# A graph network on one core: the encoder's steps without a gap, its early sums earlier, and eight source tiles of a layer's second sum moved forward

## The chip, the cores and the metric

The kernel runs on one core of a Trainium2 chip. The metric is the device time in microseconds (us) of that core, the median of several runs. The engines are PE (TensorE: matrix products, with weight loads shown as PEld), DVE (VectorE), ACT (ScalarE), POOL (GpSimd) and SP (SyncE, which here issues most DMAs; its DMA issues stand as SPq in the profile). Each engine runs its own program in order and waits on semaphores for the others.

## What is computed

3125 nodes with 128 features go through two graph networks, one after the other. Only the first is touched by the change. Cut to what matters (each edge adds its source's row to its target's row):

```python
h = relu(layernorm(x))
h = relu(h @ enc_w1.T + enc_b1) @ enc_w2.T + enc_b2          # the encoder
for w in conv_w:                                             # 5 layers
    agg = segment_sum((h @ w)[src], dst)
    gi, gh = agg @ gru_wih.T + gru_bih, h @ gru_whh.T + gru_bhh
    r, z = sigmoid(gi_r + gh_r), sigmoid(gi_z + gh_z)
    n = tanh(gi_n + r * gh_n)
    h = (1 - z) * n + z * h
x = x + sigmoid(decoder(relu(h)))
x = x + second_network(relu(layernorm(x)))                   # two sparse sums, 128 to 256 to 128
```

## The kernel before, in words

The graph is held as a dense matrix of edge counts, `AT` (source by target, fp8), so that each sum over edges is a row of matrix products. There are 25 **tiles** of up to 128 source nodes (`T`, the last, `FT` = 24, has 53), and 7 **chunks** of 4 tiles as targets (`NC` = 7, `TC` = 4; chunks 0 to 5 have 512 nodes, chunk 6 has 53). A sum for one chunk takes 49 products: every tile's state is split in a high and a low half (`H16`, f16), the last tile's stand in one. Sums are counted over the layers by q = layer x 7 + chunk.

**The first stage** builds `AT` in 40 **blocks** (b = 0 to 39, `NBT`) of 16 windows. In block b the DVE compares keys into one-hot matrices (`onehots(b)`, the pair of L877 instructions), the PE multiplies them (`windows(b)`, L1205, 16 products; it waits for `onehots_ready` >= b+1), and the ACT copies the counts into `AT` (L1583, two instructions, written out behind the products). The DVE may be up to 4 blocks ahead. Other work is hung on these blocks by hand-written tables:

- The encoder's steps. `step(b)` tells which of 16 steps stands in block b. In step 2s the PE transposes chunk s of the input (L1226) and multiplies chunk s-1 by the second weight (`enc2`, L1234, into the bank `EC2`, PSUM bank 7). In step 2s+1 it multiplies chunk s by the first weight (`enc1`, L1239) and transposes the encoded chunk s-1 (L1247). The ACT has a copy or an activation behind each (L1637, L1620, L1630, L1642). Before, step b+1 stands in blocks -1 to 6, block 7 (`REST`) has none, and step b stands in blocks 8 to 15.
- The DVE's share, placed by `block_of`, the inverse of `step`: statistics of chunk n (`first_norm(n)`: L839, L842, L851, then a power on POOL, L733) behind `onehots` of block `block_of[2n] - 2`, its normalization (L894) one block later, and the low half of an encoded chunk (`low_encoded(n)`, L903) behind `onehots` of `block_of[2n + 5]`. Each such piece stands ahead of the next block's `onehots` on the DVE.
- Keys. `KEYS_AT = {5: 1, 12: 2, 20: 3, 28: 4}`: the DVE works out a set of 128 key columns in block 5, 12, 20, 28 (L860 to L867); the PE transposes it one block later (`transposed_keys`, L1193, into the same bank `EC2`), and the ACT copies it out (`copied_keys`, L1597) behind that block's copy of the counts. An `enc2` product writes that bank, so it waits until all sets whose block lies before its own are copied:

```python
pe.wait_ge(keys_copied, 1 + sum(k < block_of[off] for k in KEYS_AT))
nc.tensor.matmul(PS[EC2][:, 0:w1], enc2, rS[:, 0:w1], start=True, stop=True).then_inc(enc2_product, 1)
```

- Sums of the first layer, as far as their sources are encoded: `PART[b]` lists `(q, t0, t1)`, the tiles t0 to t1-1 of sum q, put behind the encoder's step of block b (L1342, two products a tile). In all, the 40 blocks hold the sums 0 to 3 and a part of sum 4, in both versions.

The PE's order in a block is: windows, a transpose of keys if there is one, the encoder's step, a product of combined weights (blocks 2 to 6, L1214), the parts of sums.

**The layers.** For layers 1 to 4 the sum of chunk 0 (`aggregate`, L1260) takes its sources in groups of 4 tiles as they arrive by DMA transposes from `yS` to `H16` (L604 and L607 for chunks 0 to 5, L611 for chunk 6; semaphores `state_moved[0]` to `[6]`). Ahead of group g, `between(g)` may put other work: at g = 2 the gates of the last chunk of the layer before (`gates`, L1273 to L1284). Then comes the sum of chunk 1, then the gates of chunk 0, and so on. Two PSUM banks take turns for the sums.

Of the kernel before, what the change touches and what calls it, by code (L numbers as in the profile page):

```python
# [5 lines left out]
def gnn_kernel(nc, x, src, dst, edges, row_ends, enc_w1T, enc_b1, enc_w2T, enc_b2, conv_wT, gru_wihT, gru_whhT,  # L6
# [10 lines left out]
    P = 128  # L17
    GP = 125
    PM = GP // 16 * 16
    T = N // GP  # L20
# [37 lines left out]
    TC = 4  # L58
    CH = [(t, min(TC, T - t)) for t in range(0, T, TC)]
    NC = len(CH)  # L60
    width = lambda c: min(TC * P, N - TC * P * c)
# [11 lines left out]
    with ctx:  # L73
# [118 lines left out]
        def late(shape, dt):  # L192
            size = {F32: 4, I32: 4, F16: 2, BF16: 2}[dt]
            n = size
            for d in shape[1:]:
                n *= d
            v = carve(AT, p2[0], shape, dt)
            p2[0] += (n + 31) // 32 * 32
            return v
# [11 lines left out]
        CHECKED = 4  # L211
        FLAGGED = 20
        EARLY = 3
        OUT = late([P, TL, F], F32)
        dinvO = late([P, TL], F32)
        V16 = H16[:, 0, :, :, :]
# [6 lines left out]
        def spare(r, shape, dt):  # L223
            n = 2 if dt == F16 else 4
            for d in shape[1:]:
# [16 lines left out]
        AGG, RB, ZB, NB, IB, TB, CB = (0, 1), 2, 3, 4, 5, 6, 7  # L242
        AHEAD = 4
        ENC = -1
        REST = 7
        step = lambda b: b - ENC - (b > REST) if b != REST else None
        block_of = {step(b): b for b in range(ENC, NBT)}
        KEYS_AT = {5: 1, 12: 2, 20: 3, 28: 4}
        ROWS_AT = {7: 2, 11: 3, 15: 4}
        assert all(b + 1 < k * (PW // J) for b, k in KEYS_AT.items())  # L250
        PART = {7: [(0, 0, 4)], 8: [(0, 4, 8)], 10: [(0, 8, 12)], 12: [(0, 12, 14)], 13: [(0, 14, 16)], 14: [(0, 16, 20)],
                15: [(1, 0, 4)], 16: [(0, 20, 24)], 17: [(1, 4, 8)], 18: [(0, 24, T), (1, 8, 11)]}
        PART.update({19: [(1, 11, 14)], 20: [(1, 14, 18)], 21: [(1, 18, 21)], 22: [(1, 21, T)]})
        EVEN = [0, 4, 7, 11, 14, 18, 21, T]
        PART.update({23 + 7 * i + g: [(2 + i, EVEN[g], EVEN[g + 1])] for i in range(2) for g in range(7)})
        PART.update({37 + g: [(4, EVEN[g], EVEN[g + 1])] for g in range(NBT - 37)})
        BEGUN = EVEN[NBT - 37]
        COMB = [2 + l for l in range(L)]
        assert max(PART) < NBT
        for q in range(AHEAD + 1):  # L260
            done = [(t0, t1) for b in sorted(PART) for q1, t0, t1 in PART[b] if q1 == q]
            assert [t0 for t0, _ in done] == [0] + [t1 for _, t1 in done][:-1] and done[-1][1] == (T if q < AHEAD else BEGUN)
        EA, EB, EC2 = 6, 1, 7
        agg_bank = lambda q: PS[(0, TB, 1, CB)[q] if q < AHEAD else AGG[q % 2]]
# [30 lines left out]
        sum_ready = sem("sum_ready"); sum_copied = sem("sum_copied"); hidden_product = sem("hidden_product")  # L295
# [262 lines left out]
        def _(sp):  # L558
# [96 lines left out]
            def stored(p0, p1, u0, n0, n1):  # L655

                r = u0[1] - u0[0]
                sp.dma_start(out[n0:n1, :].rearrange("(i r) f -> i r f", r=r), OUT[p0:p1, u0[0]:u0[1], :]).then_inc(output_stored, 16)

# [40 lines left out]
        def _(pool):  # L700
# [62 lines left out]
            def low_half(c):  # L763

                pool.wait_ge(input2_hi_early, c + 1) if c < EARLY else pool.wait_ge(input2_hi, c + 1 - EARLY)
                for u0, nu, k in parts(c):
# [4 lines left out]
            for c, (t0, nt) in enumerate(CU):  # L771
                if c == 3:
                    for c1 in range(EARLY):
                        low_half(c1)
# [18 lines left out]
        def _(dve):  # L793
# [227 lines left out]
            def output_tile(u):  # L1021

                bank = PS[TILES[u % STARTED]]
                dve.wait_ge(sum2_ready, u + 1)
                link(nc.vector.scalar_tensor_tensor(OUT[:, u, :], bank[:, 0:F], dinvO[:, u:u + 1], X32[:, u, :],
                                                    ALU.mult, ALU.add))
                nc.vector.scalar_tensor_tensor(OUT[:, u, :], bank[:, F:2 * F], dinvO[:, u:u + 1], OUT[:, u, :],
                                               ALU.mult, ALU.add).then_inc(output_ready, 1)

            def decoded_tail():  # L1030
# [21 lines left out]
                for u in range(FLAGGED):  # L1052
# [11 lines left out]
                    if u == FG - 1:  # L1064
                        dve.wait_ge(sum2_transposed, 1)
                        for j in range(2):
                            k = rows2(2 * FG + j)
                            last = nc.vector.scalar_tensor_tensor(
                                OUT[0:k, 2 * FG + j, :], PS[IB][0:k, j * F:j * F + F], dinvU[0:k, 2 * FG + j:2 * FG + j + 1],
                                X32[0:k, 2 * FG + j, :], ALU.mult, ALU.add)  # L1070
# [74 lines left out]
            new_gate_input(q0 + NC - 2, NC - 2)  # L1145
            high_half(EARLY)
            new_state(q0 + NC - 2, NC - 2)
# [26 lines left out]
        def _(pe):  # L1174
# [72 lines left out]
                        last = nc.tensor.transpose(PS[EB][0:cols.shape[1], j * F:(j + 1) * F], cols, ident[:, :])  # L1247
                    last.then_inc(encoded_transposed, 1)

            def aggregate(bank, w, n0, l, ready=None, between=None):  # L1250

                for t in range(T):
                    if between is not None and t % TC == 0:
                        between(t // TC)
                    if ready is not None and t % TC == 0:
                        pe.wait_ge(*ready(t // TC))
                    if t == FT and l == 0:
                        pe.wait_ge(tail_doubled, 32 * (n0 // (TC * P) + 1))
                    for h in range(2 if t < FT else 1):
                        last = nc.tensor.matmul(bank[:, 0:w], H16[:, l % 2, t, h, :], AT3[:, t, n0:n0 + w],  # L1260
                                                start=(t == 0 and h == 0), stop=(t == T - 1))
                return last

            def gates(l, q, c):

                n0, w = CH[c][0] * P, width(c)
                H = HT[:, n0:n0 + w]
                cl = comb[:, l % 2, :]

                if q == 0:  # L1270
                    pe.wait_ge(weights_loaded, 8 * 16)
                pe.wait_ge(reset_gate, q) if q else pe.wait_ge(window_bank_free, NGR)
                nc.tensor.matmul(PS[RB][:, 0:w], whh[:, 0:F], H, start=True, stop=False)  # L1273
                pe.wait_ge(update_gate, q) if q else pe.wait_ge(window_bank_free, NGR)
                nc.tensor.matmul(PS[ZB][:, 0:w], whh[:, F:2 * F], H, start=True, stop=False)  # L1275
                pe.wait_ge(reset_hidden, q) if q else pe.wait_ge(window_bank_free, NGR)
                nc.tensor.matmul(PS[NB][:, 0:w], whh[:, 2 * F:G], H, start=True, stop=True).then_inc(hidden_product, 1)  # L1277
                pe.wait_ge(sum_copied, q + 1)
                if c == 0:
                    pe.wait_ge(comb_loaded[l % 2], 16 * (l // 2 + 1))  # L1280
                nc.tensor.matmul(PS[RB][:, 0:w], cl[:, 0:F], aggS[:, 0:w], start=False, stop=True).then_inc(reset_product, 1)  # L1281
                nc.tensor.matmul(PS[ZB][:, 0:w], cl[:, F:2 * F], aggS[:, 0:w], start=False, stop=True).then_inc(update_product, 1)  # L1282
                pe.wait_ge(new_input, q) if q else None
                nc.tensor.matmul(PS[IB][:, 0:w], cl[:, 2 * F:G], aggS[:, 0:w], start=True, stop=True).then_inc(input_product, 1)  # L1284
# [28 lines left out]
            def last_chunks(l):  # L1313

                def step(g):
                    if g == 2:
                        gates(l, (l + 1) * NC - 1, NC - 1)
                return step


# [28 lines left out]
            for b in range(NBT):  # L1349
# [5 lines left out]
                if b in COMB:  # L1355
                    combine(COMB.index(b))
                for q, t0, t1 in PART.get(b, []):
                    aggregate_part(q, t0, t1)


            for l in range(L):
                for c in range(NC):
                    q = l * NC + c
                    if q == AHEAD:
                        aggregate_part(q, BEGUN, T)
                    if AHEAD < q:
                        n0, w = CH[c][0] * P, width(c)
                        if q >= 2:
                            pe.wait_ge(sum_copied, q - 1)
                        ready = between = None  # L1370
                        if c == 0 and l >= 1:
                            ready = lambda g: (state_moved[g], (32 if g < NC - 1 else 16) * l)
                            between = last_chunks(l - 1)
                        aggregate(agg_bank(q), w, n0, l, ready=ready, between=between).then_inc(sum_ready, 1)
                    if l == L - 1 and 2 <= c < NC - 1:
                        decode1(c - 2)
                    if 1 <= c <= NC:
                        gates(l, q - 1, c - 1)
                    if l == L - 1 and c == 1:
                        permute_scales()  # L1380
                    if l == L - 1 and c == NC - 1:
                        decode1(c - 2)
                    if l == L - 1 and 2 <= c < NC - 1:
                        decode2(c - 2)
# [120 lines left out]
            n0, w = CH[NC - 1][0] * P, width(NC - 1)  # L1505
# [25 lines left out]
        def _(act):  # L1531
# [174 lines left out]
            for l in range(L):  # L1706
                for c in range(NC + 2 if l < L - 1 else NC):
# [29 lines left out]
                    if l == L - 1 and 2 <= c < NC:  # L1737
                        decode_sig(c - 2)
                        if c == NC - 2:
                            act.wait_ge(sum_ready, L * NC)  # L1740
                            for c1 in range(EARLY):
                                u0, nu = CU[c1]
# [82 lines left out]
```

## Time and profile before

| | us |
|---|---|
| median of 3 runs | 737.01 (736.59 to 737.25) |
| the profiled execution | 736.87 |
| its span in the trace | 735.0 |
| PE busy in the span | 720.2 |
| DVE busy | 331.2 |
| ACT busy | 316.5 |
| granted clock | 0.999 |

The profiled execution is 1.87 us longer than its span, and 0.14 us below the median. The span is cut by the work: up to about 125 us the 40 blocks; from there to 565.5 us the five layers; then the decoder and the second network. PE busy counts the product's own duration with its pipeline; where the PE is never starved, the starts of its instructions tell the pace better than their durations.

### The profile page before, as it was taken

To read this page: it belongs to the slowest core of one execution; us is meant where nothing else is said; L and a number is where in the kernel's file an instruction comes from. 1 tells how busy PE (TensorE), PEld (TensorE's weight loads), DVE (VectorE), ACT (ScalarE), POOL (GpSimd) and SP (SyncE) were. 2 spreads that over 40 slices of the span, in tenths; PEclk is the share of its full clock that TensorE was granted. 3 is DMA by queue.
4 is the path that set the end of the run, shared out by engine and by line. 5 is a ranking of instruction groups with operands and counts; after the bars stand their busy time and mean duration, and the time that the engine had idled before them with its cause. 6 is when DMAs were issued, how large, how long until landed. Compare 5 with 4: busy or idle time off the path is not lost.

```text
span 735.0 us, 9911 instructions
## 1 busy us (share of the span) xinstructions
PE 720.2 (98%) x4071; PEld 394.7 (54%) x4071; DVE 331.2 (45%) x665; ACT 316.5 (43%) x467; POOL 43.6 (6%) x57
## 2 busy tenths in 40 slices
PE   6989999999999999999999999999999999999998
PEld 4556666445444444444444444544445545558887
DVE  7999997625023241123331222655644642122532
ACT  5978877736244344234452333433446421122000
POOL 4230000000000000000000000120002220000000
PEclk9999999999999999999999999999999999999999
DMA  6020000835003222021230213520001100000100
GB/s 170 3 92 10 3 4 3 156 62 84 8 1 62 62 47 45 1 48 38 53 78 0 49 37 38 94 86 2 1 0 54 53 1 1 1 1 3 37 25 31
DMA packets 79239, 28.39 MB, mean 39 GB/s; under 512 B 70519, under 2 KB 78390, under 8 KB 79062
## 3 DMA queue, kind: packets, MB, share of 16 engines
q1 hardware_dynamic: 78230, 26.93, 17.3%
q8 instruction: 33, 0.54, 0.3%
q0 software_dynamic: 240, 0.66, 0.3%
q10 hardware_dynamic: 720, 0.13, 0.1%
q14 instruction: 16, 0.13, 0.1%
HBM read 8.03 MB, written 2.60 MB: 14 GB/s over the span
## 4 chain that ended last, share of the span: by engine, by line
PE 89%; DVE 6%; DMA 2%; ACT 1%; SPq 1%; issue 0%; POOL 0%; ACTq 0%; DVEq 0%
PE PSA L1260 35%; PE PSA L1477 9%; PE PSA L1421 8%; PE PSA L1342 7%; PE PSA L1205 4%; PE PSA L1273 4%; PE PSA L1282 4%; PE PSA L1281 4%; PE PSA L1277 4%; PE PSA L1275 4%; PE PSA L1284 3%; DVE CT L877 3%; PE PSA L1409 2%; PE PSA L1397 1%; DMA H<-yS 1%; PE PSA L1301 1%
## 5 line engine op out<-in xcount | busy, mean ns | idle before, releaser
L1260 PE MATMUL PSA<-AT,H 128*128 128x512 fp8e3 (+1 forms) x1470 | 275.8, 347 | 0.3 <-DMA H<-yS 0.2
L1260 PEld LDWEIGHTS PSA<-AT,H 128*128 128x128 f16 x1470 | 126.7, 98 | 151.5 <-issue 12.0
L1090 DVE SCALAR_TENSOR_TENSOR rS<-PSA,bias,rS 128x512 f32<-128x512 f32 (+1 forms) x35 | 23.9, 682 | 261.1 <-ACT rS L1659 261.1
L1659 ACT ACTIVATE rS<-PSA,bias 128x512 f32<-128x512 f32 (+1 forms) x35 | 22.1, 632 | 198.0 <-PE PSA L1281 197.9
L1583 ACT ACTIVATE AT<-PSA 128x1000 fp8e3<-128x1000 f32 (+1 forms) x79 | 74.5, 999 | 18.6 <-PE PSA L1205 18.3
L1557 ACT ACTIVATE CTL<-AT 128x3125 fp8e3<-128x3125 fp8e3 (+1 forms) x25 | 69.9, 2797 | 0.0
L1421 PE MATMUL PSA<-CT,H 128*128 128x512 fp8e3 (+1 forms) x336 | 65.3, 351 | 0.1
L1477 PE MATMUL PSA<-AT,CT 128*128 128x256 f16 x576 | 64.9, 273 | 0.0
L1477 PEld LDWEIGHTS PSA<-AT,CT 128*128 128x128 fp8e3 x576 | 55.5, 98 | 6.5 <-issue 0.2
L1342 PE MATMUL PSA<-AT,H 128*128 128x512 fp8e3 x245 | 58.0, 379 | 0.0
L1205 PEld LDWEIGHTS PSA<-CT 128*128 128x128 bf16 x625 | 40.2, 99 | 16.3 <-DVE CT L877 8.9
L877 DVE TENSOR_TENSOR CT<-CT 128x2048 bf16<-128x2048 bf16 x40 | 48.6, 1215 | 0.0
L1205 PE MATMUL PSA<-CT 128*128 128x125 bf16 x625 | 44.6, 224 | 3.5 <-DVE CT L877 3.5
L1421 PEld LDWEIGHTS PSA<-CT,H 128*128 128x128 f16 x336 | 29.4, 98 | 33.9 <-issue 1.9
L877 DVE TENSOR_TENSOR CT<-yS,CT 128x2000 bf16<-128x2000 bf16 x40 | 47.6, 1191 | 0.0
L1342 PEld LDWEIGHTS PSA<-AT,H 128*128 128x128 f16 x245 | 23.1, 98 | 23.8 <-issue 2.3
L1273 PE MATMUL PSA<-HT,whh 128*128 128x512 f32 (+1 forms) x70 | 32.7, 548 | 0.0
L1277 PE MATMUL PSA<-HT,whh 128*128 128x512 f32 (+1 forms) x70 | 32.6, 547 | 0.0
L1284 PE MATMUL PSA<-aggS,comb 128*128 128x512 f32 (+1 forms) x70 | 32.6, 547 | 0.0
L1281 PE MATMUL PSA<-aggS,comb 128*128 128x512 f32 (+1 forms) x70 | 32.6, 547 | 0.0
L1275 PE MATMUL PSA<-HT,whh 128*128 128x512 f32 (+1 forms) x70 | 32.6, 547 | 0.0
L1282 PE MATMUL PSA<-aggS,comb 128*128 128x512 f32 (+1 forms) x70 | 32.6, 547 | 0.0
(186 smaller groups left out, 662.3 us busy)
## 6 DMA issues: line engine op xcount, KB each, us to landing
AT<-scale_scratch SPq DMA_DIRECT2D x1, 1562.5 KB, 6.5
H<-in_x SPq DMA_DIRECT2D x1, 1536.0 KB
out<-AT SPq DMA_DIRECT2D x12, 128.0 KB
comb_scratch<-CT SPq DMA_DIRECT2D x1, 960.0 KB, 4.6
comb<-comb_scratch SPq DMA_DIRECT2D x5, 192.0 KB, 2.6
H<-yS SPq DMA_TRANSPOSE x48, 2.5
H<-in_x SPq DMA_DIRECT2D x1, 512.0 KB, 5.0
CT<-AT SPq DMA_TRANSPOSE x25, 4.0
```

The lines of the kernel that those rows point to most:

```text
L877: last = nc.vector.tensor_tensor(oh, io.unsqueeze(1).to_broadcast([SL, GW, n_, 2]), pairs.unsqueeze(2).to_broadcast([SL, GW, n_, 2]), ALU. ...
L1205: last = nc.tensor.matmul(PS[2 + 2 * g + w // 4][:, (w % 4) * 128:(w % 4) * 128 + W * T], ohP[b % BL][:, j // 2, :, j % 2], ohK[b % BL][:, ...
L1260: last = nc.tensor.matmul(bank[:, 0:w], H16[:, l % 2, t, h, :], AT3[:, t, n0:n0 + w], start=(t == 0 and h == 0), stop=(t == T - 1))
L1273: nc.tensor.matmul(PS[RB][:, 0:w], whh[:, 0:F], H, start=True, stop=False)
L1275: nc.tensor.matmul(PS[ZB][:, 0:w], whh[:, F:2 * F], H, start=True, stop=False)
L1277: nc.tensor.matmul(PS[NB][:, 0:w], whh[:, 2 * F:G], H, start=True, stop=True).then_inc(hidden_product, 1)
L1281: nc.tensor.matmul(PS[RB][:, 0:w], cl[:, 0:F], aggS[:, 0:w], start=False, stop=True).then_inc(reset_product, 1)
L1342: last = nc.tensor.matmul(agg_bank(q)[:, 0:w], H16[:, 0, t, h, :], AT3[:, t, n0:n0 + w], start=(t == 0 and h == 0), stop=(t == T - 1))
L1421: nc.tensor.matmul(PS[bank][:, 0:w], halves[:, u, h, :], CT2[:, u // 2, n0:n0 + w, u % 2], start=(u == 0 and h == 0), stop=False)
L1477: nc.tensor.matmul(PS[TILES[u % STARTED]][:, 0:2 * F], CT2[:, s // 2, nodes(u), s % 2], Z16[:, s, :, :].rearrange("p h f -> p (h f)"), sta ...
L1557: nc.scalar.activation(junk[0:k, :], AT3[0:k, t, 0:N], ACT.Copy, saturate=False, accum_out=deg[0:k, t:t + 1]).then_inc(degree_summed, 1)
L1583: nc.scalar.activation(AT3[0:P, :, w0 * W:(w0 + gw) * W].rearrange("p t (w d) -> p t w d", w=gw), counts[:, 0:gw, 0:W * T].rearrange("p w ...
```

## The change

In the first stage block 7 is no longer left out: step b+1 stands in block b for all 16 steps, so the steps 8 to 15 come one block sooner (blocks 7 to 14), and with them the DVE's pieces for chunks 4 to 6 and the low halves of chunks 2 to 6. The table `PART` follows: its parts of sums 0 and 1 are cut differently and end in blocks 17 and 22. In the layers 1 to 4 the first 8 tiles of the sum of chunk 1 (16 products) are issued ahead of the sixth group (g = 5) of the sum of chunk 0; the sum of chunk 1 then takes the rest (33 products) at its old place.

```diff
+        EARLY_TILES = 2 * TC
...
-        REST = 7
-        step = lambda b: b - ENC - (b > REST) if b != REST else None
+        step = lambda b: b - ENC
...
-        PART = {7: [(0, 0, 4)], 8: [(0, 4, 8)], 10: [(0, 8, 12)], 12: [(0, 12, 14)], 13: [(0, 14, 16)], 14: [(0, 16, 20)],
-                15: [(1, 0, 4)], 16: [(0, 20, 24)], 17: [(1, 4, 8)], 18: [(0, 24, T), (1, 8, 11)]}
-        PART.update({19: [(1, 11, 14)], 20: [(1, 14, 18)], 21: [(1, 18, 21)], 22: [(1, 21, T)]})
+        PART = {7: [(0, 0, 4)], 8: [(0, 4, 8)], 9: [(0, 8, 12)], 11: [(0, 12, 16)], 13: [(0, 16, 20)], 14: [(1, 0, 4)],
+                15: [(0, 20, 24)], 16: [(1, 4, 8)], 17: [(0, 24, T), (1, 8, 10)]}
+        PART.update({18 + i: [(1, 10 + 3 * i, 13 + 3 * i)] for i in range(5)})
...
-            def aggregate(bank, w, n0, l, ready=None, between=None):
+            def aggregate(bank, w, n0, l, ready=None, between=None, t0=0, t1=T):
...
-                for t in range(T):
+                for t in range(t0, t1):
...
                 def step(g):
                     if g == 2:
                         gates(l, (l + 1) * NC - 1, NC - 1)
+                    if g == NC - 2:
+                        q = (l + 1) * NC + 1
+                        pe.wait_ge(sum_copied, q - 1)
+                        aggregate(agg_bank(q), width(1), CH[1][0] * P, l + 1, t1=EARLY_TILES)
                 return step
...
-                        aggregate(agg_bank(q), w, n0, l, ready=ready, between=between).then_inc(sum_ready, 1)
+                        aggregate(agg_bank(q), w, n0, l, ready=ready, between=between,
+                                  t0=EARLY_TILES if c == 1 and l >= 1 else 0).then_inc(sum_ready, 1)
```

Three places show how the instructions move. The lines of the changed file are 5 higher behind `aggregate` (L1342 is L1346, L1583 is L1588).

The PE in block 13 and at the begin of block 14, before (L1193 is the transpose of key set 2, L1239 and L1247 the encoder's step 13, L1234 with 53 columns its step 14):

```order
L1193 MATMUL PSA<-ident,CT 128x128 [waits keys_ready,state_encoded]
L1193 MATMUL PSA<-ident,CT 128x128
L1239 MATMUL PSA<-aggS,CT 128x53 [waits x_copied]
L1247 MATMUL PSA<-ident,HT 128x128 [waits encoded_lo,state_encoded]
L1247 MATMUL PSA<-ident,HT 128x128 x3
L1342 MATMUL PSA<-AT,H 128x512 [waits encoded_lo]
L1342 MATMUL PSA<-AT,H 128x512 x3
L1205 MATMUL PSA<-CT 128x125 [waits window_bank_free,onehots_ready]
```

The same place now:

```order
L1193 MATMUL PSA<-ident,CT 128x128 [waits keys_ready,state_encoded]
L1193 MATMUL PSA<-ident,CT 128x128
L1234 MATMUL PSA<-rS,CT 128x53 [waits keys_copied,state_encoded,enc1_relu]
L1346 MATMUL PSA<-AT,H 128x512 [waits encoded_lo]
L1346 MATMUL PSA<-AT,H 128x512 x7
L1205 MATMUL PSA<-CT 128x125 [waits window_bank_free,onehots_ready]
```

Step 13 has gone to block 12, step 14 has come up from block 14, and it now stands directly behind the transpose of the keys, with the wait for `keys_copied`.

The DVE behind block 5's keys (L867 is the last of them), before:

```order
L867 SCALAR_TENSOR_TENSOR CT<-CT 128x128 [waits starts_subtracted]
L877 TENSOR_TENSOR CT<-CT 128x2048 [waits windows_counted]
L877 TENSOR_TENSOR CT<-yS,CT 128x2000
L839 BN_STATS stat<-H 128x6 [waits x_loaded1]
L839 BN_STATS stat<-H 128x6 x3
L842 BN_AGGR mv<-stat 128x2 [waits vector_chain]
L842 BN_AGGR mv<-stat 128x2 x3
L851 TENSOR_SCALAR mv<-mv 128x4 [waits vector_chain]
L903 SCALAR_TENSOR_TENSOR H<-PSA,H 128x4x128 [waits encoded_hi]
```

The same place now:

```order
L867 SCALAR_TENSOR_TENSOR CT<-CT 128x128 [waits starts_subtracted]
L839 BN_STATS stat<-H 128x6 [waits x_loaded1]
L839 BN_STATS stat<-H 128x6 x3
L842 BN_AGGR mv<-stat 128x2 [waits vector_chain]
L842 BN_AGGR mv<-stat 128x2 x3
L851 TENSOR_SCALAR mv<-mv 128x4 [waits vector_chain]
L877 TENSOR_TENSOR CT<-CT 128x2048 [waits windows_counted]
L877 TENSOR_TENSOR CT<-yS,CT 128x2000
L894 TENSOR_SCALAR H<-H,mv,lnsc 128x128 [waits roots_ready]
L894 TENSOR_SCALAR H<-H,mv,lnsc 128x128 x3
L903 SCALAR_TENSOR_TENSOR H<-PSA,H 128x4x128 [waits encoded_hi]
```

The statistics of chunk 4 now stand ahead of block 6's one-hots, and its normalization right behind them.

The PE at a layer's begin, before:

```order
L1260 MATMUL PSA<-AT,H 128x512 [waits state_moved4]
L1260 MATMUL PSA<-AT,H 128x512 x7
L1260 MATMUL PSA<-AT,H 128x512 [waits state_moved5]
L1260 MATMUL PSA<-AT,H 128x512 x7
L1260 MATMUL PSA<-AT,H 128x512 [waits state_moved6]
L1260 MATMUL PSA<-AT,H 128x512 [waits sum_copied]
L1260 MATMUL PSA<-AT,H 128x512 x48
```

And now:

```order
L1260 MATMUL PSA<-AT,H 128x512 [waits state_moved4]
L1260 MATMUL PSA<-AT,H 128x512 x7
L1260 MATMUL PSA<-AT,H 128x512 [waits sum_copied]
L1260 MATMUL PSA<-AT,H 128x512 x15
L1260 MATMUL PSA<-AT,H 128x512 [waits state_moved5]
L1260 MATMUL PSA<-AT,H 128x512 x7
L1260 MATMUL PSA<-AT,H 128x512 [waits state_moved6]
L1260 MATMUL PSA<-AT,H 128x512 [waits sum_copied]
L1260 MATMUL PSA<-AT,H 128x512 x32
```

16 of the 49 products of chunk 1's sum stand ahead of the wait for the sixth chunk's state.

## Rows read from the trace of the kernel before

**Rows 1.** The page's busy times: us, share of the span, instructions.

```profile
PE 720.2 (98%) x4071; PEld 394.7 (54%) x4071; DVE 331.2 (45%) x665; ACT 316.5 (43%) x467; POOL 43.6 (6%) x57
```

**Rows 2.** Timeline of PE, blocks 7 to 15: start, us, instruction, [idle before, releaser].

```profile
37.65 1.13 PE L1205 MATMUL PSA<-CT 128*128 128x125 bf16 x16 [0.88 <-DVE CT L877]
38.61 1.89 PE L1342 MATMUL PSA<-AT,H 128*128 128x512 fp8e3 x8
41.40 1.12 PE L1205 MATMUL PSA<-CT 128*128 128x125 bf16 x16 [0.90 <-DVE CT L877]
42.36 0.60 PE L1226 MATMUL PSA<-ident,H 128*128 128x128 f32 x4
...
43.66 1.89 PE L1342 MATMUL PSA<-AT,H 128*128 128x512 fp8e3 x8
45.39 1.11 PE L1205 MATMUL PSA<-CT 128*128 128x125 bf16 x16
...
48.91 1.13 PE L1205 MATMUL PSA<-CT 128*128 128x125 bf16 x16 [1.06 <-DVE CT L877]
...
58.43 1.12 PE L1205 MATMUL PSA<-CT 128*128 128x125 bf16 x16
59.39 0.39 PE L1193 MATMUL PSA<-ident,CT 128*128 128x128 f32 x2
59.61 0.32 PE L1239 MATMUL PSA<-aggS,CT 128*128 128x53 f32 x2
...
60.23 1.03 PE L1342 MATMUL PSA<-AT,H 128*128 128x512 fp8e3 x4
61.27 1.13 PE L1205 MATMUL PSA<-CT 128*128 128x125 bf16 x16
62.23 0.37 PE L1234 MATMUL PSA<-rS,CT 128*128 128x53 f32 x2
62.45 1.89 PE L1342 MATMUL PSA<-AT,H 128*128 128x512 fp8e3 x8
64.17 1.11 PE L1205 MATMUL PSA<-CT 128*128 128x125 bf16 x16
```

**Rows 3.** Timeline of DVE, pieces between the one-hots of blocks 6 to 14.

```profile
33.27 0.86 DVE L839 BATCH_NORM_STATS2 stat<-H 128x6 f32<-128x128 f32 x4
...
34.67 0.68 DVE L903 SCALAR_TENSOR_TENSOR H<-PSA,H 128x512 f16<-128x512 f32 x1
35.27 1.21 DVE L877 TENSOR_TENSOR CT<-CT 128x2048 bf16<-128x2048 bf16 x1
...
37.99 1.11 DVE L894 TENSOR_SCALAR H<-H,mv,lnsc 128x128 f32<-128x128 f32 x4
39.01 1.22 DVE L877 TENSOR_TENSOR CT<-CT 128x2048 bf16<-128x2048 bf16 x1
...
58.29 0.68 DVE L903 SCALAR_TENSOR_TENSOR H<-PSA,H 128x512 f16<-128x512 f32 x1
```

**Rows 4.** Timeline of ACT: a copy of encoder input in block 8, the keys' in block 13.

```profile
44.45 0.60 ACT L1637 ACTIVATE aggS<-PSA 128x512 f32<-128x512 f32 x1
...
60.90 0.39 ACT L1597 ACTIVATE CT<-PSA 128x256 bf16<-128x256 f32 x1
```

**Rows 5.** Timeline of PE, the sums at the begin of layers 1, 3 and 4.

```profile
184.91 12.69 PE L1260 MATMUL PSA<-AT,H 128*128 128x512 fp8e3 x58 [0.22 <-DMA H<-yS]
...
373.63 17.86 PE L1260 MATMUL PSA<-AT,H 128*128 128x512 fp8e3 x82
...
470.57 18.10 PE L1260 MATMUL PSA<-AT,H 128*128 128x512 fp8e3 x82
```

**Rows 6.** Timeline of ACT at the begin of layer 1, behind the first sum.

```profile
187.55 2.80 ACT L1557 ACTIVATE CTL<-AT 128x3125 fp8e3<-128x3125 fp8e3 x1
```

**Rows 7.** Timelines of DVE and POOL around block 4: statistics, power, normalization.

```profile
26.50 1.11 DVE L894 TENSOR_SCALAR H<-H,mv,lnsc 128x128 f32<-128x128 f32 x4
...
24.42 1.91 POOL L733 TENSOR_TENSOR lnsc<-mv,mhalf 128x4 f32<-128x4 f32 x1 [5.00 <-DVE mv L851]
```

## The prediction

> **What bounds the kernel now.** The page's busy times come first: the PE is busy for 720.2 of 735.0 us [rows 1], and neither version has other products than the other (4071 are in the trace). So only time in which the PE stands still can be won or lost, and the question is where it does. The second view is the PE's timeline with its idle times. In the blocks 7 to 13 it waits for the one-hots of the DVE: 0.88, 0.90 and 1.06 us ahead of the windows of blocks 7, 8 and 10 [rows 2]. From block 14 on every product follows on the one before; the DVE is ahead by then. The third place is a layer's begin. Of layers 1 to 4, layer 1 shows 0.22 us of waiting for the DMA of the state [rows 5], and in layer 4 the same 82 products take 18.10 us where layer 3's take 17.86, so 0.24 us more [rows 5]. Layers 2 and 3 show none.
>
> **The layer's begin.** 16 products are put ahead of the wait for the sixth chunk's state. A product takes 0.216 us (8 between 43.66 and 45.39, [rows 2]), so 16 take 3.45 us, and the waits of 0.22 and 0.24 us vanish under them. That is **-0.46 us**. I look for what is late next. The last source (chunk 6's state) also has 3.45 us more. The new wait for `sum_copied` asks for the sum whose copy the gates at g = 2 have already waited for, so nothing stands behind it. The first sum's end comes 3.45 us later, and the gates that need its copy come after 33 products instead of 49: 7.1 us. In these the ACT has one copy (some 0.6 us, as its other 512-column copies [rows 4]) and one instruction of 2.80 us [rows 6], so cover of 3.7 us remains. The gates themselves stay at their old place in the count of products, and DVE, ACT and SP see them unmoved. Bounds: no gain at all if other executions have no wait there, up to some 1 us if all four layers have one like these two.
>
> **The DVE's stream in the first stage.** Nothing is added, but pieces stand ahead of earlier one-hots. From rows 3: statistics of a chunk 1.40 us (33.27 to 34.67), a low half 0.60 (34.67 to 35.27), a normalization 1.02 (37.99 to 39.01). The one-hots of block 6 come 1.40 us later (statistics of chunk 4 ahead of them). Those of block 7 come 1.02 later (the statistics were ahead of them anyway, the normalization is new). Those of block 8 come 1.40 later, and those of block 12 at their old time, since by then both orders hold the same. Block 13 has the low half of chunk 4 newly ahead, which before stood behind it at 58.29 [rows 3]: 0.60 us later.
>
> **The PE up to block 13.** Windows 7 start at 37.65 + 1.02 = 38.67. The block then holds windows 0.96 (37.65 to 38.61), the encoder's step 8 of 1.30 (42.36 to 43.66, before in block 8) and 8 products of 1.73, and ends at 42.66. Windows 8 wait for the DVE until 41.40 + 1.40 = 42.80. Before, the time from windows 8 to windows 13 was 58.43 - 41.40 = 17.03 us with 1.06 of idling in it [rows 2], so 15.97 of work. Now this stretch loses step 8 (1.30), gains step 13 (0.62, from 59.61 to 60.23) and 4 more products of a sum (0.86): 16.15 us. From 42.80 that is 58.95, just short of the DVE's 58.43 + 0.60 = **59.03**, at which windows 13 start. They start 0.60 later than before, with 0.62 + 0.86 = 1.48 us more work already done: up to here the PE is ahead by **0.88 us**. The idle times of blocks 7 to 10 are used, as the change's parts stand in them; a new one of up to 1.4 us at block 6 is paid in it.
>
> **Block 13, the new wait.** Here a step goes wrong. The `enc2` product of step 14 now stands in block 13, directly behind the transpose of key set 2, and both use bank `EC2`. Its wait counts the sets of blocks before 13, so it includes set 2, which the ACT copies only behind its two copies of block 13's counts. Before, step 14 stood one block later and windows 14 lay between; it started at 62.23 without idling [rows 2]. The ACT's copy of the keys starts 60.90 - 58.43 = 2.47 us after windows 13 start and takes 0.39 [rows 2, 4], so it ends 2.86 after. The PE reaches the product after windows 0.96 and transpose 0.22 (59.39 to 59.61), 1.18 after. It stands for 2.86 - 1.18 = **1.68 us**. Bounds: 1.5, were the ACT's result seen at the start of its next instruction, and 2.0, were the first weight load after the wait seen in full. Queued behind the wait on the PE are 8 products of sum 0, ready since long, and windows 14. The PE's rows stand in the program's order throughout, so I let none of them fill the wait. From the ACT's side nothing hangs on the PE at that moment, so the wait ends.
>
> **After it.** Before, the PE stood 61.27 - 60.23 - 4 x 0.216 = 0.18 us ahead of windows 14 [rows 2]. Now windows 14 start at 59.03 + 2.86 + 0.22 (62.23 to 62.45) + 1.73 = 63.84, and the DVE has their one-hots by 61.27, so this idle time is gone. Measured against windows 15, which before came at 64.17: the new order has still block 14's windows (0.96) to go at 63.84, then 64.80, with step 14 and 40 products of sums done in both. That is **+0.63 us** (-0.88 + 1.68 - 0.18 = +0.62, the same by the parts). Beyond, the DVE's order is the same but for a low half in block 14 and 16, the PE never waited from windows 14 on and now comes later still, so the DVE's lead grows; and the total of `PART` up to block 22 is unchanged. Nothing gives the 0.63 back.
>
> **Sum.** +0.63 - 0.46 = +0.17 us. The profiled execution's 736.87 becomes 737.04; on the median of 737.01 it is **737.2 us**. I take the rows' values for both terms.
>
> **Rivals.**
> (1) *The wait in block 13 is hidden*: the ACT copies the keys before the PE gets there, for instance since the windows 13 are held back more than I think and the PE reaches the product late. For it: the wait is one in a list of three and I infer its end from one row. Against it: the ACT's copy always follows the windows by two copies of counts, whatever moment they start. Time: the +0.63 becomes -1.06 and the sum -1.52: 735.5 us.
> (2) *The layer's gain is another*: the DMA landing varies by execution. With none of it 737.6; with 1 us 736.6.
> (3) *Slower: the ACT hands over the encoder's input too late.* In block 8 the product of step 9 waits for the ACT's copy from block 7. Before, this copy ended at 44.45 + 0.60 = 45.05, 3.65 us after its block's windows (41.40) [rows 2, 4]; now 38.67 + 3.65 = 42.32, against the PE's arrival at 42.80 + 0.96 = 43.76. The slack is 1.44 us, and it decides if the copy is later by more than that. In this case the idle times of blocks 8 and 10 (0.90 + 1.06, [rows 2]) are not won: +2.0, so 739.1 us.
> (4) *Slower: POOL's power comes late.* Statistics, one-hots and normalization of chunk 4 now follow on each other, with the power on POOL (1.91 us) beside the one-hots. The same order stands already for chunk 3: the power runs from 24.42 to 26.33, and the normalization starts at 26.50 without a wait [rows 7]. If POOL could not run beside the one-hots, the power would start behind them, the normalization and all one-hots from block 7 to 13 would be 1.9 us late, and the time 739.1 us as well.
> The Trainium skill, "SBUF — State Buffer", section on practical consequences, says that a VectorE instruction with two SBUF inputs and a GpSimd one that reads SBUF exclude each other, whoever started first keeping the port. By that rule rival 4 would be the outcome. The trace does not agree: the power at 24.42 started inside the DVE's pair and was done before it ended.
>
> **Chances.** The forecast 0.73; rival 1 0.08; rival 2 0.11 (half of it to each side); rival 3 0.05; rival 4 0.03. A difference below 0.2% (1.5 us) can't be told from none in a measurement of this kernel. Faster by more needs rival 1 with the layer's gain in full, which sits on the border: 0.05. Slower by more needs rival 3 or 4: 0.08. The rest, 0.87, lies within. The range has the forecast and rival 2 with the spread of the runs (0.3 either side), and on the low side rival 1: 735.5 to 738.3 us.
>
> **What would show it.** In the changed profile: an idle time of 1.5 to 2.0 us ahead of L1234 in block 13, put down to ACT's L1597 (copy of the keys), at about 60.2 us; windows 13 starting near 59.0 and windows 14 near 63.8; no idle time by L1205 in blocks 8 to 12 above 0.2 us; one of about 1.4 us ahead of windows 6; no wait for `yS` at L1260. The last L1205 some 0.6 us later than before. I am wrong if L1234 doesn't wait in block 13, if the PE waits for ACT's L1637 in blocks 8 or 10, or if the gates after a layer's first sum begin to wait for the ACT.

## The result and the profile after

The changed kernel took 739.56 us (median of 9 runs, 737.9 to 739.82) against 736.9 us before (9 runs, 736.59 to 737.25): a ratio of 1.003 with a 95% interval of 1.0022 to 1.0039. It is slower by some 2.7 us, where 737.2 us and a range of 735.5 to 738.3 had been forecast. The profiled execution took 739.12 us with a span of 737.3 (before 735.0).

The nine runs fall in two groups. Seven have a mean granted clock of 0.998 and lie at 739.12 to 739.82 us; two have 1.000 and lie at 737.9 and 738.32. The profiled run is of the first kind. This will turn out to be the larger part of the miss.

The page's busy times, and the PE's timeline at the places of [rows 2] (start, us, instruction, [idle before, releaser]):

```profile
PE 720.9 (98%) x4071; PEld 395.8 (54%) x4071; DVE 331.4 (45%) x665; ACT 316.6 (43%) x467; POOL 45.9 (6%) x57
```

```profile
34.63 1.13 PE L1205 MATMUL PSA<-CT 128*128 128x125 bf16 x16 [1.24 <-DVE CT L877]
...
38.49 1.13 PE L1205 MATMUL PSA<-CT 128*128 128x125 bf16 x16 [0.57 <-DVE CT L877]
...
42.63 1.12 PE L1205 MATMUL PSA<-CT 128*128 128x125 bf16 x16
...
58.86 1.29 PE L1205 MATMUL PSA<-CT 128*128 128x125 bf16 x16 [0.22 <-DVE CT L877]
59.98 0.39 PE L1193 MATMUL PSA<-ident,CT 128*128 128x128 f32 x2
62.33 0.40 PE L1234 MATMUL PSA<-rS,CT 128*128 128x53 f32 x2 [1.96 <-ACT CT L1602]
62.56 2.90 PE L1346 MATMUL PSA<-AT,H 128*128 128x512 fp8e3 x8
65.25 1.75 PE L1205 MATMUL PSA<-CT 128*128 128x125 bf16 x16
66.84 0.32 PE L1247 MATMUL PSA<-ident,nS 128*117 128x128 f32 x1
67.00 1.89 PE L1346 MATMUL PSA<-AT,H 128*128 128x512 fp8e3 x8
68.72 1.12 PE L1205 MATMUL PSA<-CT 128*128 128x125 bf16 x16
```

The waits of [rows 2] ahead of the windows of blocks 8 and 10 are gone, and one of 1.24 us ahead of windows 6 is new. In block 13 the PE waits 1.96 us ahead of L1234 for the ACT's copy of the keys. What is new against the forecast are the two lines behind it: 8 products take 2.69 us (62.56 to 65.25), where 8 of them take 1.72 from 67.00 (67.00 to 68.72), and windows 14 take 1.59 instead of 0.95. The view of stretches gives the granted clock there (columns: stretch, its length, busy us and count of PE, PEld, DVE, ACT, POOL, then the clock, DMA share, GB/s):

```profile
60.00:62.30 2.30, 0.36 (x5) 0.13 (x3) 2.30 (x3) 2.18 (x4) 0.00 (x0) 1.00 0.05 12
62.30:64.00 1.70, 1.67 (x8) 0.83 (x9) 1.70 (x3) 0.54 (x2) 0.00 (x0) 0.79 0.00 0
64.00:66.00 2.00, 2.00 (x12) 1.18 (x11) 1.96 (x5) 0.00 (x0) 1.36 (x1) 0.50 0.00 0
66.00:68.00 2.00, 2.00 (x17) 1.48 (x16) 0.62 (x1) 1.66 (x2) 0.32 (x1) 0.82 0.26 66
```

From some moment between 62.3 and 64 the granted clock is at its lower level of 1.2 GHz (0.50), and it returns between 66 and 68 us. Before that the PE had been idle for 1.96 us. In narrower stretches the clock is 1.00 up to 63.1 us and 0.50 from 63.3, so it fell about 1 us after the PE had begun to work again at 62.33: the first products behind the wait still run at full pace.

The layers' begins, to be read beside [rows 5]: no wait for `yS` is left, the 82 products take 17.86 us in layer 1 and in layer 4.

```profile
182.29 17.86 PE L1260 MATMUL PSA<-AT,H 128*128 128x512 fp8e3 x82
...
473.13 17.86 PE L1260 MATMUL PSA<-AT,H 128*128 128x512 fp8e3 x82
```

The ACT around block 13's windows (the L1588 at 57.54 belong to block 12, L1625 and L1647 to step 13, the L1588 at 59.98 to block 13, and L1602 is the copy of the keys):

```profile
57.54 1.90 ACT L1588 ACTIVATE AT<-PSA 128x1000 fp8e3<-128x1000 f32 x2 [0.79 <-PE PSA L1205]
59.32 0.31 ACT L1625 ACTIVATE rS<-PSA,bias 128x53 f32<-128x53 f32 x1
59.51 0.61 ACT L1647 ACTIVATE H<-PSA 128x512 f16<-128x512 f32 x1
59.98 1.92 ACT L1588 ACTIVATE AT<-PSA 128x1000 fp8e3<-128x1000 f32 x2
61.75 0.43 ACT L1602 ACTIVATE CT<-PSA 128x256 bf16<-128x256 f32 x1
```

**The books of the profiled execution.** At the first product of the layers (L1273) the changed kernel is 2.95 us late: it starts at 128.94, before at 125.99. I had forecast 0.63. The difference, piece by piece, from the rows above and the same view elsewhere:

| | us |
|---|---|
| forecast for the first stage | +0.63 |
| the whole stage runs earlier from block 5 on (30.32 against 30.50), where the ten traces spread from 30.32 to 31.12 | -0.18 |
| windows 13 take 1.12 instead of 0.96: their second half waits for the ACT's copy of block 12 | +0.16 |
| the wait ahead of L1234 is 2.13 (62.33 - 58.86 - 1.12 - 0.22), not 1.68 | +0.45 |
| the lower clock: 2.69 - 1.73 and 1.59 - 0.95 | +1.60 |
| windows behind the two blocks with 5 products (17 and 22) take 1.09 instead of 0.95 | +0.28 |
| sum | +2.94 |

The pieces miss the 2.95 by 0.01. The layers then give back 0.63: at the gates behind layer 4's first two sums the distance is 490.83 - 488.51 = 2.32 us, and the spans differ by 2.3.

### The profile page after: what moved, and what is told of

Its sections match the earlier page's. It is cut to its first block, busy times and chain, and to the rows that moved or that the text cites. A ratio compares the mean times of both kernels' runs of the same rounds, so it can differ in the third digit from the quotient of the medians.

```text
span 737.3 us, 9911 instructions
## 1 busy us (share of the span) xinstructions
PE 720.9 (98%) x4071; PEld 395.8 (54%) x4071; DVE 331.4 (45%) x665; ACT 316.6 (43%) x467; POOL 45.9 (6%) x57
## 4 chain that ended last, share of the span: by engine, by line
PE 88%; DVE 7%; ACT 2%; POOL 1%; issue 1%; DMA 1%; SPq 0%; ACTq 0%; DVEq 0%
PE PSA L1260 37%; PE PSA L1482 9%; PE PSA L1346 7%; PE PSA L1426 5%; PE PSA L1205 4%; PE PSA L1273 4%; PE PSA L1284 3%; PE PSA L1281 3%; PE PSA L1282 3%; PE PSA L1277 3%; PE PSA L1275 3%; DVE CT L877 2%; PE PSA L1414 2%; PE PSA L1402 1%; DVE stat L839 1%
## 5 line engine op out<-in xcount | busy, mean ns | idle before, releaser
L1588 ACT ACTIVATE AT<-PSA 128x1000 fp8e3<-128x1000 f32 (+1 forms) x79 | 74.5, 1000 | 20.8 <-PE PSA L1205 20.4
L1346 PE MATMUL PSA<-AT,H 128*128 128x512 fp8e3 x245 | 59.0, 384 | 0.0
L877 DVE TENSOR_TENSOR CT<-CT 128x2048 bf16<-128x2048 bf16 x40 | 48.7, 1217 | 0.9 <-ACT CT L1602 0.9
L877 DVE TENSOR_TENSOR CT<-yS,CT 128x2000 bf16<-128x2000 bf16 x40 | 47.7, 1192 | 0.0
L1346 PEld LDWEIGHTS PSA<-AT,H 128*128 128x128 f16 x245 | 23.2, 99 | 24.3 <-issue 2.8
L1273 PE MATMUL PSA<-HT,whh 128*128 128x512 f32 (+1 forms) x70 | 32.7, 548 | 0.0
```

The source lines that it names most:

```text
L877: last = nc.vector.tensor_tensor(oh, io.unsqueeze(1).to_broadcast([SL, GW, n_, 2]), pairs.unsqueeze(2).to_broadcast([SL, GW, n_, 2]), ALU. ...
L1346: last = nc.tensor.matmul(agg_bank(q)[:, 0:w], H16[:, 0, t, h, :], AT3[:, t, n0:n0 + w], start=(t == 0 and h == 0), stop=(t == T - 1))
L1588: nc.scalar.activation(AT3[0:P, :, w0 * W:(w0 + gw) * W].rearrange("p t (w d) -> p t w d", w=gw), counts[:, 0:gw, 0:W * T].rearrange("p w ...
```

## The experiments

The theory: the wait in block 13 is the cause, first by itself and then by the lower clock behind it; the rest of the change is a gain. The rivals: the DVE's pieces moved ahead cost it, the layers' begin costs it, or the products behind the wait are slow for another reason than the clock. Each group of four ran beside the kernel before on one chip (737.26 us in the first, 737.17 in the second), and the ratios refer to that.

**The two halves of the change.** The layer part alone:

```diff
-        step = lambda b: b - ENC
+        REST = 7
+        step = lambda b: b - ENC - (b > REST) if b != REST else None
...
(PART as before)
```

> The kernel before with the layer part of the change alone. My theory after reading both traces: the waits at the begin of layers 1 and 4 were 0.39 and 0.24 us, so it is 0.6 us faster than before (736.3 us, ratio 0.9991). The rival that the early products cost as much as they save (a late copy of the first sum) expects no difference or slower.

Measured: 736.77 us, ratio 0.9995 (0.9986 to 1.0004). The median is 0.49 us under the kernel before; by the interval that can't be told from none. In its trace the waits for `yS` are gone, and both sums take 17.86 us. In the trace of before the PE's gap in layer 1 was larger than the printed idle time: 24 products from 179.34 end their issue at 184.52, the next starts at 184.91. So the gain is 0.39 + 0.24 = 0.63 us by the traces, and they show no new wait there.

The first stage alone:

```diff
                     if g == 2:
                         gates(l, (l + 1) * NC - 1, NC - 1)
-                    if g == NC - 2:
-                        q = (l + 1) * NC + 1
-                        pe.wait_ge(sum_copied, q - 1)
-                        aggregate(agg_bank(q), width(1), CH[1][0] * P, l + 1, t1=EARLY_TILES)
```

> The first stage of the change alone, the layers as before. My theory: the whole loss is in the first stage, +2.9 us where the clock falls behind the wait in block 13: 740.1 us at a mean granted clock of 0.998, and some 1.6 us less in runs where it doesn't fall. The rival that part of the loss came from the layers expects under 739.6.

Measured: 739.54 us, ratio 1.0034 (1.0022 to 1.0046). Three runs at a clock of 0.998 lie at 740.2 to 740.34, three at 1.000 at 738.48 to 738.89. I had set the rival's bound at 739.6, and the median lies 0.06 us under it; but it falls between two groups of three, so it decides nothing. Group by group the medians are 740.25 and 738.69, and those of the whole change 739.59 and 738.11 (first measurement): with the layers as before the kernel is some 0.6 us slower, which is their gain. So the whole loss is in the first stage. The profiled execution is one at 1.000, which shows the same wait without the slow products:

```profile
62.62 0.40 PE L1234 MATMUL PSA<-rS,CT 128*128 128x53 f32 x2 [1.96 <-ACT CT L1598]
62.86 1.89 PE L1342 MATMUL PSA<-AT,H 128*128 128x512 fp8e3 x8
64.58 1.11 PE L1205 MATMUL PSA<-CT 128*128 128x125 bf16 x16
```

**The wait taken away, by two ways.** First the key set goes to block 11, so that it is copied out in block 12:

```diff
-        KEYS_AT = {5: 1, 12: 2, 20: 3, 28: 4}
+        KEYS_AT = {5: 1, 11: 2, 20: 3, 28: 4}
```

> The changed kernel with key set 2 worked out in block 11 instead of 12, so that it is copied out in block 12 and step 14 in block 13 doesn't wait for it. My theory: the wait of 2.1 us and the slower clock behind it (1.6 us) both vanish, and the gain of the filled idle times comes out: 1.2 us in the first stage and 0.6 in the layers under the kernel before, 735.2 us, clock 1.000. The rival that the loss comes from the DVE's pieces moved ahead, or from the copies of the ACT, expects it to stay above 736.9.

Measured: 736.04 us, ratio 0.9985 (0.9976 to 0.9994). The wait is gone (L1234 at 60.08, directly behind windows 13 at 58.95), the clock is 1.000 in all 11 runs, and the kernel is faster than before. The DVE's moved pieces and the early products of the layers are still in this kernel, so neither is the cause of the loss. But the gain is 1.2 us, not the 1.8 I expected. Most of the missing part is in blocks 17 to 22, where the PE now comes early enough to meet the next limits:

```profile
72.24 1.25 PE L1205 MATMUL PSA<-CT 128*128 128x125 bf16 x16
73.33 1.46 PE L1346 MATMUL PSA<-AT,H 128*128 128x512 fp8e3 x6
...
77.82 1.46 PE L1346 MATMUL PSA<-AT,H 128*128 128x512 fp8e3 x6
79.31 1.12 PE L1205 MATMUL PSA<-CT 128*128 128x125 bf16 x16
...
83.80 1.26 PE L1205 MATMUL PSA<-CT 128*128 128x125 bf16 x16
84.89 1.89 PE L1346 MATMUL PSA<-AT,H 128*128 128x512 fp8e3 x8
```

The windows at 72.24 and 83.80, behind blocks with 5 products, take 1.09 us to the next start instead of 0.95, and 6 products from 77.82 (1.29 us) are followed at 79.31, 0.20 late, by windows that the DVE holds, behind the keys of block 20. That is 0.48 of the missing 0.6 us.

Second, the encoder leaves out block 13 instead, so that steps 14 and 15 stand in blocks 14 and 15 as before, with the key sets unmoved:

```diff
-        step = lambda b: b - ENC
+        REST = 13
+        step = lambda b: b - ENC - (b > REST) if b != REST else None
```

> The changed kernel with block 13 left out by the encoder (steps 14 and 15 back in blocks 14 and 15), key sets as they were. No product stands between the keys' transpose and their copy in the same bank. Like the run with key set 2 in block 11: no wait, clock 1.000, 736.0 us, 1.2 us under the kernel before. If the gain of that run came from moving the keys themselves, this one stays above 736.9.

Measured: 735.94 us, ratio 0.9982 (0.9973 to 0.9991), none of the 11 runs at 0.998. So it is the product standing between the keys' transpose and their copy that costs, not where the keys are worked out. Its median is the lowest of all versions, but its interval and that of the run before overlap, so the two can't be told apart.

**The wait kept, its idling filled.** 9 products into an unused bank (the result doesn't use them) stand ahead of the waiting one:

```diff
+                    if off == 14:
+                        pe.wait_ge(enc1_relu, NC)
+                        for i in range(9):
+                            nc.tensor.matmul(PS[EA][:, 0:512], H16[:, 0, i % 4, 0, :], AT3[:, i % 4, 0:512],
+                                             start=True, stop=True)
                     pe.wait_ge(keys_copied, 1 + sum(k < block_of[off] for k in KEYS_AT))
```

> The changed kernel with 9 products of 512 columns (1.94 us) into an unused bank put into the wait of block 13 (they add work that the result doesn't use). My theory: the wait itself stays as long, but the PE is busy in it, so the clock stays up: 738.0 us, 1.6 us under the changed kernel, clock 1.000, and the 8 products behind the wait at 0.216 us each. The rival that these products are slow for another reason (PSUM or operands just written) expects them slow still and 739.6 us.

Measured: 738.01 us, ratio 1.0011 (1.0002 to 1.002), no run at 0.998. The waiting product (L1239 in this file) starts at 62.37, as late as in the changed kernel (62.33), but the 8 products behind it are at full pace:

```profile
60.34 2.11 PE L1236 MATMUL PSA<-AT,H 128*128 128x512 fp8e3 x9
62.37 0.43 PE L1239 MATMUL PSA<-rS,CT 128*128 128x53 f32 x2
62.64 1.89 PE L1351 MATMUL PSA<-AT,H 128*128 128x512 fp8e3 x8
64.36 1.11 PE L1205 MATMUL PSA<-CT 128*128 128x125 bf16 x16
```

So with added work the kernel is faster than its own executions at 0.998, by the price of the lower clock, and the rival of slow operands or banks falls. The same with 4 products:

```diff
-                        for i in range(9):
+                        for i in range(4):
```

> The changed kernel with 4 products (0.86 us) in the wait of block 13 instead of 9, so that some 1.3 us of it stay idle. The idle time of 1.24 us ahead of windows 6 had no slower product behind it, so I expect the clock to stay at 1.000 and 738.0 us, as with 9. The rival that any wait at this place slows the products behind it expects 739.6 us.

Measured: 738.0 us, ratio 1.0011 (1.0002 to 1.002), all 11 runs at 1.000. The trace has an idle time of 1.01 us ahead of the waiting product, and no slower one behind it. The two fillings cost the same. The copy of the keys is as late as before in both; what differs is how long the PE idles, and with it whether the clock falls.

**The change once more:**

> The changed kernel itself, once more, beside the others of this group on one chip. It should show two groups of times, one at a mean granted clock of 0.998 and one at 1.000, some 1.6 us apart (about 739.7 and 738.1), the slower one more often; were the clock not the cause, the two would not go with it.

Measured: 738.25 us, ratio 1.0023 (1.0012 to 1.0035). Four runs at 1.000 lie at 737.9 to 738.25, three at 0.998 at 739.76 to 740.05, and none lies between. I had expected the slower group more often. Which one holds the median changes: here the faster one, in the first measurement the slower. The profiled execution is one at 1.000 and has the same wait of 1.96 us as the first one:

```profile
62.91 0.40 PE L1234 MATMUL PSA<-rS,CT 128*128 128x53 f32 x2 [1.96 <-ACT CT L1602]
63.15 1.89 PE L1346 MATMUL PSA<-AT,H 128*128 128x512 fp8e3 x8
64.88 1.12 PE L1205 MATMUL PSA<-CT 128*128 128x125 bf16 x16
```

**The light blocks filled up.** Key set 2 in block 11, and the parts of sum 1 cut otherwise:

```diff
-        PART = {7: [(0, 0, 4)], 8: [(0, 4, 8)], 9: [(0, 8, 12)], 11: [(0, 12, 16)], 13: [(0, 16, 20)], 14: [(1, 0, 4)],
-                15: [(0, 20, 24)], 16: [(1, 4, 8)], 17: [(0, 24, T), (1, 8, 10)]}
-        PART.update({18 + i: [(1, 10 + 3 * i, 13 + 3 * i)] for i in range(5)})
+        PART = {7: [(0, 0, 4)], 8: [(0, 4, 8)], 9: [(0, 8, 12)], 11: [(0, 12, 16)], 13: [(0, 16, 20)], 14: [(1, 0, 3)],
+                15: [(0, 20, 24)], 16: [(1, 3, 6)], 17: [(0, 24, T), (1, 6, 9)]}
+        PART.update({18 + i: [(1, 9 + 3 * i, 12 + 3 * i)] for i in range(4)})
+        PART.update({22: [(1, 21, T)]})
```

> The version with key set 2 in block 11, with the parts of sum 1 cut so that blocks 17 to 22 hold 7, 6, 6, 6, 6, 7 products instead of 5, 6, 6, 6, 6, 5 (blocks 14 and 16 hold 6 instead of 8). In the 5-product blocks the windows behind took 1.09 us instead of 0.95, waiting for the ACT's copies, and block 21 waited 0.20 us for the DVE. Theory: two or three of these 0.14 to 0.20 us vanish, 735.7 us. The rival that the DVE sets the pace of blocks 17 to 22 anyway expects no difference, 736.0.

Measured: 736.15 us, ratio 0.9984 (0.9975 to 0.9993): no gain over 736.04. The waits for the ACT are gone, and the one for the DVE ahead of windows 21 has grown. From start to start it is 0.65 us (79.66 - 77.72 - 1.29) instead of 0.20. The PE comes there earlier by the wait for the ACT behind block 17 and by two products (0.43 us) that now stand behind it, and it stops at the same windows:

```profile
77.72 1.46 PE L1347 MATMUL PSA<-AT,H 128*128 128x512 fp8e3 x6
79.66 1.12 PE L1206 MATMUL PSA<-CT 128*128 128x125 bf16 x16 [0.47 <-DVE CT L878]
```

The rival was right: in this version the one-hots of the DVE set the pace up to block 21, and the table of parts decides only where the PE waits for them.

## Why the prediction was wrong

**Right.** That the first stage decides, and that in block 13 the `enc2` product waits behind the keys' transpose for the ACT. The DVE's stream came out within 0.01 us: windows 13 start 0.61 us later than before (forecast 0.60), taken from windows 5 in both traces (58.86 - 30.32 = 28.54 against 58.43 - 30.50 = 27.93). The PE's books up to block 13 held too: in the trace it is ready ahead of windows 13 and waits 0.22 us for the DVE. Rivals 3 and 4 did not happen: L1239 has no wait in blocks 8 and 10, and the normalization of chunk 4 starts at 34.49, directly behind its block's one-hots. Of rival 1 the wait stayed, but its price was right in kind: with the wait taken away the kernel is 1.2 us faster than before, against the forecast's 1.5.

**Right in its outcome, wrong in its reading: POOL beside the one-hots.** From the power that starts at 24.42 and is done before the DVE's pair ends [rows 7] the prediction reads that the trace disagrees with the Trainium skill. The durations agree with it. In the trace of before the same power also stands once beside L903, which has one operand in PSUM:

```profile
34.84 1.01 POOL L733 TENSOR_TENSOR lnsc<-mv,mhalf 128x4 f32<-128x4 f32 x1 [8.50 <-DVE mv L851]
```

It takes 1.01 us there, and 1.91 at 24.42, where it starts beside the first L877 of a pair, with two operands in SBUF. In all ten traces the powers of four columns that start so end 0.94 to 0.96 us after the second L877 starts (24.42 + 1.91 = 26.33 against 25.38), as if each were held until the first L877 had ended; the L877 keep their usual 1.22 and 1.19 us. This is what the Trainium skill says in "SBUF — State Buffer", section "Who interferes with whom": of two such instructions the one that comes second is blocked until the other is done. What rival 4 had wrong is the length: the power is held for one instruction of the pair and not for both, 0.90 us and not 1.9. In the changed kernel it starts at 32.41 and ends at 34.32, only 0.17 us before the normalization. This is read from durations, and those on POOL are rough; no run here moved a power by itself. The page's busy times fit: POOL's rise by 2.3 us, 0.90 by this power and 1.46 by two gathers (L725) that now start beside an L877 (1.72 and 1.68 us instead of 0.99 and 0.95).

**Wrong, the wait's length** ("It stands for 2.86 - 1.18 = 1.68 us"; measured 2.13, beyond the bound of 2.0 too). I took the ACT's delay behind windows 13 from a block in which the ACT was free when the windows came. With step 13 in block 12 the ACT still has its two instructions to do, until 59.98, and starts the copies 1.12 us behind the windows' start instead of 0.68. The 0.16 us inside windows 13 has another cause. Block 12 has no products of a sum, so windows 13 start 1.99 us behind windows 12 (56.87 to 58.86), and their second half waits for the ACT's copy of block 12, which is not late itself (57.54, 0.67 behind windows 12). I had followed the DVE and the PE through the moved steps, and had taken the ACT's from one row.

**Wrong, what follows the wait** ("Now windows 14 start at 59.03 + 2.86 + 0.22 (62.23 to 62.45) + 1.73 = 63.84", and +0.63 us from there). The sum priced the 8 products and the windows behind the wait at their full pace; windows 14 start at 65.25. In the profiled execution they ran at the granted clock's lower level, +1.60 us; over all runs of the change and of its first stage alone, the two groups' medians are 1.5 to 1.7 us apart. This is the larger part of the miss, and with it alone the time leaves the range (737.2 + 1.6 = 738.8). The executions without it take 737.9 to 738.32 us, about 0.9 over the forecast, and all but the highest lie within the range. The trace of before gave no clear sign of it. There is a row of slow products behind an idle time of 2.00 us: windows 0 take 1.66 us to the next start (13.60 to 15.26), where those of later blocks take 0.95:

```profile
9.82 0.66 PE L1193 MATMUL PSA<-ident,CT 128*128 128x128 f32 x2 [1.57 <-DVE CT L867]
12.49 1.12 PE L1226 MATMUL PSA<-ident,H 128*128 128x128 f32 x4 [2.00 <-ACT H L1607]
13.60 1.86 PE L1205 MATMUL PSA<-CT 128*128 128x125 bf16 x16
15.26 2.02 PE L1239 MATMUL PSA<-aggS,CT 128*128 128x512 f32 x2
17.07 1.24 PE L1205 MATMUL PSA<-CT 128*128 128x125 bf16 x16
```

But the pair of transposes ahead of that idle time is slow already (0.66 us at 9.82, where the same pair takes 0.39 at 59.39), so the row doesn't show what an idle time does to a stretch at full pace. The granted clock is printed as 1.00 there, so I can't say either that the clock is the cause. What could be read is that from windows 0 on all idle times of the old schedule in this stage were 1.06 us or less, and the one that I added was the first near 2.

**Wrong, what is late next** ("nothing gives the 0.63 back", and no cost beyond). The light blocks 17 and 22 have 5 products. The next windows come before the ACT has emptied the banks, 0.14 us each time, as windows 13 do behind block 12. The old table had at least 6 in each of the blocks 17 to 22. I had looked at the table's total only.

**Mis-sized, the layers' gain** (0.46, by the traces 0.63). I took the printed idle time of 0.22 us in layer 1. It counts from the modelled end of the last product, so the pause in issue is 0.17 us longer. With starts and the pace of 0.216 us it comes out at 0.39.

What stays open is why the clock falls in one execution and not in the next. The wait is 1.96 us in all three traces of it, of both kinds. I did not vary its length between 1.01 and 1.96 us; the next longest idle times behind which the same traces show no slower product are 1.24 us ahead of windows 6 and up to 1.38 us ahead of the L1226 at 18.79.

## What to carry to other kernels

A step moved by one slot takes its waits along: look at which other work of the same slot shares its buffer, and follow every engine through the new order, the one that hands over too, not only the two that you suspect. An idle time on TensorE was not priced by its length alone here; look for the longest one that the old schedule had, and if a new one is longer, put slower products behind it into the range, and look whether the run times form two groups that go with the mean clock. A cover that is one product too thin is a wait (5 products waited 0.14 us, 6 did not): in a table that hands out work to slots the smallest slot counts, not the sum.

## What the runs showed of the hardware

In the one trace that shows it, the granted clock fell from 2.4 to 1.2 GHz (0.50) about 1 us after an idle time of 1.96 us had ended, and cost 1.60 us. The mean clock of 0.998 and the time say the same of 13 of 22 runs with this idle time (7 of 9, 3 of 6 and 3 of 7), at 1.5 to 1.7 us between the groups' medians, and of none of the 22 runs in which the same wait was filled so far that 1.01 us or nothing of it was left idle. The Trainium skill, "TensorE: Matmul & The Clock Gate", in its part on the clock gate, says that the slower level is the default and that activity releases it. The trace shows both levels and the return to the higher one under work; which of them is the default no run here shows. I had not expected that one program with one and the same wait would do both.
